# Down-weight sums moved behind the layer norm's scales, z spilled and loaded by halves, transfers reordered

## The chip, the cores and the metric

The kernel runs on one core of one Trainium2 chip. The metric is the device time of one execution in microseconds (us). TensorE (PE), VectorE (DVE), ScalarE (ACT) and GpSimd (POOL) compute; all transfers are issued from SyncE's queue (SP, in the profile SPq), one after the other.

## What is computed

x has 4 batches of 1024 tokens with 512 features. Two layers, each with a residual:

```python
x = x + layernorm(attn(layernorm(x), Wq, Wk, Wv, Wo))
x = x + layernorm(ffn(layernorm(x), gate_cp, up_cp, down_cp))

def attn(x, Wq, Wk, Wv, Wo):     # attention between features, not tokens
    q, k, v = x @ Wq, x @ Wk, x @ Wv
    scores = einsum('bse,bsf->bef', q, k) / sqrt(16)
    return einsum('bef,bsf->bse', softmax(scores), v) @ Wo

def ffn(h, gate_cp, up_cp, down_cp):   # 512 -> 2048 -> 512
    gate_w, up_w, down_w = (spline(cp) for cp in (gate_cp, up_cp, down_cp))
    return (silu(h @ gate_w.T) * (h @ up_w.T)) @ down_w.T
```

The three weights of the second layer are cubic (Catmull-Rom) interpolations of some 8,000 control points each, 1,048,576 values from one line of points. So gate and up are reached over short polynomials of the position: a token's 512 features are first multiplied with 16 position features per tile and per quarter of the input, which gives z, and z with small unit weights gives gate and up. The down weight is 40 columns wide boxes and a few moments, computed on the chip from control points times coefficients, four terms added.

## The kernel before, in words

There are two blocks with a barrier between them.

**The attention block** (`attention_block`, from L63) takes one batch per body: `body(b, True)` for b = 0 to 2 in a hardware loop, then `body(3, False)`, `more` being False. All products are done in a high and a low part (three matmuls for one, `product`, L690). PE's order in a body: chain products of 4 squares each (K = 4 tiles): Gram matrix times Wk, then Wq times that, softmax between, attention times Wo, Wv times that (L761 to L797), then the output of 8 token tiles (NT = 8, L801 to L810), then the Gram matrix of the next batch (`next_gram`). ScalarE evacuates the high part of a bank (`evac_hi`), VectorE the low part (`evac_lo`, L544), and PE waits for the low parts of the chain before the next chain (`lo_done`).

The layer norm of the next batch runs in body b beside the last two chains: VectorE's `ln_step(b + 1, j)` (L535) does for tile j the statistics (`ln_stats`, L517 to L520), for tile j - 1 the normalization (`ln_norm`, L522) and for j - 2 the low part (`ln_lo`, L530), one step behind each `evac_lo`. Between statistics and `ln_norm` GpSimd computes 1 / sqrt(variance + eps) with two tiny operations, `ln_scale` (L333): it waits for `ln_mv` and gives `ln_rstd`, on which `ln_norm` waits. For the output tiles `y_scale` (L341) does the same.

GpSimd also makes weights, in the order of its program (`body`, L387). `unit_weights(c)` (L351) makes the unit weights of the second layer, two of 8 parts per body; `sum_job(b, k)` (L374) makes a sixth (JOBS = 6) of a body's share of the down weight: a multiply of 640 elements per partition (L379) and two additions (L381 of 320, L385 of 160). Before, all six sums and both `unit_weights` of a body stand ahead of its eight `ln_scale`. The jobs' inputs come in two buffers, `load_job(b, k)` (L224), which waits for `job_summed` of two jobs earlier. `job_hi` (L440, ScalarE) and `job_lo` (L555, VectorE) split the sums in the output tiles' loop, and `job_ready` counts them; the store of all of a body's jobs is L290, the last of SP's body.

SP's `body` (L246) holds the order of the transfers: x tiles for the next norm (`load_x`, four buffers), jobs, the stores of the unit weights (`store_units`), then in the loop over t (L272) the stores of x1 (the first layer's output) and the residual loads (`load_res`, L212). In the last body VectorE's `ystats` and residual sums (L619, L630) run as ever, and the first five tiles' z are made: `feats.spill` writes z to DRAM, and at t = 3 `ffn_in.load_z` loads it back, turned so that features are partitions (L284 to L286). One group's z is 2 MB, in two halves of 1 MB. A spill is one transfer of 128 KB (L885 to L887), 16 of them for a group (8 per half, SPILLS = 16).

**The FFN block** (`ffn_block`, from L1031) runs 8 groups of 512 tokens, 16 steps each. A step on PE: gate and up products from z (`gate_up`, L1405), a moment pair, a sixteenth of the previous group's down products (`part`), and in some steps the z of a tile of the next group. ScalarE does silu (L1249, its table load is the only one in this block), VectorE gate times up (L1318), GpSimd the low part (L1204). Before the first step of a group PE waits for z's first half, before step 8 for the second (L1408, `i % HALF == 0`). In quad 2 of 4 of each group SP does `regroup` (L1159): it spills the next group's 16 pieces, then `load_z` (L1022) waits for the first half's spills, loads, waits for the second half's and loads. Behind it in SP's order stand an output store, the reload of a residual buffer, and the load of a token tile (`feats.load`, L878) which VectorE's `stats` (L924) reads a quad later.

## Time and profile before

| | us |
|---|---|
| Median of 3 runs | 849.83 |
| Lowest and highest | 847.49, 853.59 |
| Profiled execution, device time | 854.14 |
| Its span in the profile | 852.4 |
| PE busy | 754.2 (88%) |
| VectorE busy | 522.1 (61%) |
| GpSimd busy | 444.9 (52%) |
| ScalarE busy | 369.4 (43%) |

The attention block takes the first 422 us of the span, of which body 0 begins near 40, body 1 near 138, body 2 near 226 and body 3 near 314; the FFN block takes the rest. A row names the line of the kernel, the engine, and out<-in by tile names; a bracket at its end is the idle time of its engine before it and who ended that. In the waits the name before the arrow is the waiting engine and instruction, the one behind it who released it. PEclk is the granted TensorE clock as a share of 2.4 GHz. Some tiles share memory, so that `z`, `down`, `shared` or `z_lo` in a row of the first block are its weights, residuals and norm parts.

### The profile page before, as it was taken

What the parts mean: (1) busy time and instruction counts of PE and PEld (TensorE: products, weight loads), DVE (VectorE), ACT (ScalarE), POOL (GpSimd) and SP (SyncE); (2) the same over time, 40 slices, a digit from 0 to 9 for tenths busy, and PEclk for the clock granted to TensorE, in tenths of its full rate; (3) what the DMA queues carried; (4) which work ended last, traced back from release to release, by engine and by line L of the source; (5) the groups of instructions that cost most, each with busy time, mean ns of one, the idle gap of its engine ahead of it and who ended that gap; (6) DMA issues with size and microseconds to landing.
All of it is one profiled execution on the core that took longest, in us unless ns stands there. A gap on an engine that the chain in (4) does not pass through costs nothing.

```text
span 852.4 us, 19230 instructions
## 1 busy us (share of the span) xinstructions
PE 754.2 (88%) x7152; PEld 511.4 (60%) x7152; DVE 522.1 (61%) x1025; ACT 369.4 (43%) x632; POOL 444.9 (52%) x616
## 2 busy tenths in 40 slices
PE   5696699999999999799577799989979899998996
PEld 3484476877687768586333465656646556564565
DVE  6553663586448754565466477766757767764553
ACT  2321232333233323233356465655656556665641
POOL 4299547934793479203235344554535545454542
PEclk9798699999999999899779899999999999999999
DMA  8444426521764165405843326262361633516212
GB/s 283 151 161 128 150 88 243 184 94 65 218 206 115 52 202 196 105 1 157 280 143 113 124 74 213 77 222 90 122 202 57 195 122 124 200 65 199 76 61 100
DMA packets 64313, 120.54 MB, mean 141 GB/s; under 512 B 12144, under 2 KB 28656, under 8 KB 62192
## 3 DMA queue, kind: packets, MB, share of 16 engines
q1 hardware_dynamic: 64240, 119.53, 42.9%
q8 instruction: 51, 0.84, 0.4%
q14 instruction: 22, 0.18, 0.1%
HBM read 82.94 MB, written 36.57 MB: 140 GB/s over the span
## 4 chain that ended last, share of the span: by engine, by line
PE 25%; SPq 9%; DMA 7%; DVE 4%; issue 3%; ACT 2%; POOL 0%; DVEq 0%; ACTq 0%
SPq L886 8%; DMA z<-token_features 5%; PE gbank L1417 5%; PE ubank L1417 4%; PE ybank L1458 3%; PE ybank L1459 2%; PE ybank L1460 2%; PE mbank L1433 2%; DMA out<-x_res 1%; PE ybank L1447 1%; DVE inter L1318 1%; PE ybank L1449 1%; PE ybank L1448 1%; PE zbank L974 1%; ACT gated L1249 1%
## 5 line engine op out<-in xcount | busy, mean ns | idle before, releaser
L1204 POOL TENSOR_TENSOR act<-inter,act 128x512 f16<-128x512 f32 x128 | 156.5, 1230 | 154.9 <-ACT act L1245 154.9
L1318 DVE SCALAR_TENSOR_TENSOR inter<-ubank,c_up,gated 128x512 f32<-128x512 f32 x128 | 95.9, 749 | 107.1 <-ACT gated L1249 99.8
L1249 ACT ACTIVATE gated<-gbank,c_gate 128x512 f32<-128x512 f32 x128 | 87.7, 685 | 71.2 <-PE gbank L1417 71.1
L1458 PE MATMUL ybank<-down,act 128*128 128x160 f16 x512 | 111.3, 236 | 0.0
L1459 PE MATMUL ybank<-down,act 128*128 128x160 f16 x512 | 110.4, 235 | 0.0
L1460 PE MATMUL ybank<-down,act 128*128 128x160 f16 x512 | 110.3, 235 | 0.0
L1245 ACT CAST act<-inter 128x512 f16<-128x512 f32 x128 | 78.9, 617 | 47.4 <-DVE inter L1318 47.4
L1417 PE MATMUL gbank<-z,s_twice 128*32 128x512 f16 x512 | 52.9, 403 | 30.4 <-DMA z<-token_features 18.1
L1458 PEld LDWEIGHTS ybank<-down,act 128*128 128x128 f16 x512 | 50.3, 98 | 40.4 <-issue 36.7
L692 PE MATMUL ybank<-ga_hi,xT_hi 128*128 128x512 f32 x128 | 52.8, 412 | 3.8 <-ACT shared L490 1.9
L1417 PE MATMUL ubank<-z,s_twice 128*32 128x512 f16 x512 | 51.9, 395 | 2.7 <-DVE inter L1318 2.7
L345 POOL TENSOR_TENSOR yr<-ymv,eps 128x1 f32<-128x1 f32 x32 | 20.5, 639 | 64.0 <-DVE ymv L622 64.0
L490 ACT ACTIVATE shared<-ybank,yr 128x512 f32<-128x512 f32 x32 | 22.0, 688 | 72.9 <-POOL yr L347 72.9
L1459 PEld LDWEIGHTS ybank<-down,act 128*128 128x128 f16 x512 | 50.6, 99 | 3.9 <-issue 0.3
L547 DVE SCALAR_TENSOR_TENSOR tu_lo<-chain,tu_hi 128x512 fp32r<-128x512 f32 x32 | 22.1, 690 | 50.3 <-ACT tu_hi L432 50.3
L1417 PE MATMUL gbank<-z,s_low 128*32 128x512 f16 x512 | 51.8, 395 | 0.0
L1417 PE MATMUL ubank<-z,s_low 128*32 128x512 f16 x512 | 51.6, 393 | 0.0
L1460 PEld LDWEIGHTS ybank<-down,act 128*128 128x128 f16 x512 | 50.5, 99 | 0.0
L693 PE MATMUL ybank<-ga_lo,xT_hi 128*128 128x512 f32 x128 | 50.1, 392 | 0.0
L694 PE MATMUL ybank<-ga_hi,xT_lo 128*128 128x512 f32 x128 | 50.0, 390 | 0.0
L432 ACT ACTIVATE tu_hi<-chain 128x512 fp32r<-128x512 f32 x32 | 19.1, 596 | 69.9 <-PE chain L694 69.9
L1417 PEld LDWEIGHTS gbank<-z,s_twice 128*32 128x32 f16 x512 | 13.3, 93 | 58.4 <-issue 31.4
(190 smaller groups left out, 2110.4 us busy)
## 6 DMA issues: line engine op xcount, KB each, us to landing
x_ln<-x SPq DMA_DIRECT2D x64, 256.0 KB, 3.5
z<-token_features SPq DMA_DIRECT2D x16, 1024.0 KB, 6.5
job<-job_in SPq DMA_DIRECT2D x24, 640.0 KB, 5.0
shared<-x SPq DMA_DIRECT2D x32, 256.0 KB, 2.7
x<-shared SPq DMA_DIRECT2D x32, 256.0 KB, 2.0
token_features<-z_hi SPq DMA_DIRECT2D x64, 128.0 KB
token_features<-z_lo SPq DMA_DIRECT2D x64, 128.0 KB
x_res<-x SPq DMA_DIRECT2D x32, 256.0 KB, 2.7
```

The source lines that it names most:

```text
L692: pe.matmul(out, l_hi, r_hi, start=start, stop=False)
L693: pe.matmul(out, l_hi, r_lo, start=False, stop=False)
L694: return pe.matmul(out, l_lo, r_hi, start=False, stop=stop)
L886: sp.dma_start(self.spilled[half, part, k].rearrange("f t n -> t f n"), self.z_parts[buf][part][:, half * self.K + k, :]).then_inc(self.z_ ...
L1204: pool.tensor_tensor(hidden[par][:, i, TOK:2 * TOK], inter[:, i % INTERS, :], hidden[par][:, i, 0:TOK], ALU.subtract).then_inc(inter_ready, 1)
L1245: act.copy(hidden[par][:, i, 0:TOK], inter[:, i % INTERS, :]).then_inc(inter_hi_done, 1)
L1249: act.activation(gated[:, slot % 2, :], gbank[:], ACT.Silu, scale=c_gate[:]).then_inc(silu_done, 1)
L1318: dve.scalar_tensor_tensor(out=inter[:, i % INTERS, :], in0=ubank[:], scalar=c_up[:], in1=gated[:, i % 2, :], op0=ALU.mult, op1=ALU.mult). ...
L1417: mm = pe.matmul(bank[rows], part[:, side, c, w, rows], z[par][:, i // 4 * 4 + u, :], start=start, stop=not start)
L1458: pe.matmul(out, hidden[par][:, r, high], box[:, 0], start=False, stop=False)
L1459: pe.matmul(out, hidden[par][:, r, high], box[:, 1], start=False, stop=False)
L1460: mm = pe.matmul(out, hidden[par][:, r, low], box[:, 0], start=False, stop=False)
```

## The change

1. GpSimd, bodies 0 to 2: the order is now `unit_weights`, jobs 0 and 1, `unit_weights`, and then behind the eight `ln_scale` one after the other the multiply of job 2, its additions, the multiply of job 3 and so on to job 5. The last body keeps its order.
2. SP, bodies 0 to 2: jobs 2 and 3 are loaded behind the first `store_units`; jobs 4 and 5 between the x tiles 4 to 7; the next body's jobs 0 and 1 behind them.
3. SP, last body: z's halves are loaded at t = 4 and t = 5, and no longer both at t = 3, so behind the last residual load; the store of the down-weight jobs goes ahead of the last x1 store.
4. ScalarE does one tiny silu at the end of the last body.
5. `regroup` spills one half and loads it, then the other.

```diff
@@ -135,6 +135,7 @@
         srec = sb("srec", [P, K], F32)
         mhalf = sb("mhalf", [P, 1], F32)
         eps = sb("eps", [P, 1], F32)
+        silu_seen = sb("silu_seen", [P, 1], F32)
         carrier = sb("carrier", [P, 1], F32)
 
 
@@ -251,18 +252,26 @@
                     sp.wait_ge(xn_normed, B * NT)
                     for m in range(XR):
                         feats.load(sp, x1_t, m, m)
-                load_job(b, 2)
-                load_job(b, 3)
+                if not more:
+                    load_job(b, 2)
+                    load_job(b, 3)
                 store_units(2 * b, True)
-                load_job(b, 4)
-                load_job(b, 5)
+                if more:
+                    load_job(b, 2)
+                    load_job(b, 3)
+                else:
+                    load_job(b, 4)
+                    load_job(b, 5)
                 store_units(2 * b + 1, more)
                 if more:
+                    load_x(b + 1, XR)
+                    load_x(b + 1, XR + 1)
+                    load_job(b, 4)
+                    load_x(b + 1, XR + 2)
+                    load_x(b + 1, XR + 3)
+                    load_job(b, 5)
                     load_job(b + 1, 0)
                     load_job(b + 1, 1)
-                if more:
-                    for t in range(XR, NT):
-                        load_x(b + 1, t)
                 else:
 
                     sp.wait_ge(s_stored, (2 * B + 1) * 64)
@@ -270,6 +279,9 @@
                     ffn_in.load_units(sp, s_dram, KF)
                     feats.spill(sp, 0, SPILLS // 2, 0)
                 for t in range(NT):
+                    if not more and t == NT - 1:
+                        sp.wait_ge(job_ready, (b + 2) * JOBS)
+                        sp.dma_start(d_dram[b], job_out[:]).then_inc(d_stored, 16)
                     sp.wait_ge(x1_ready, b * NT + t + 1)
                     sp.dma_start(x1_t[b * NT + t], x_res[:, t % XR, :]).then_inc(x1_stored[t % XR], 16)
                     if 1 <= t <= NT - XR:
@@ -281,13 +293,15 @@
                         feats.load(sp, x1_t, XR + t, t)
                     if not more and t < 2:
                         feats.spill(sp, (t + 2) * SPILLS // 4, (t + 3) * SPILLS // 4, 0)
-                    if not more and t == 3:
+                    if not more and t == 4:
                         sp.wait_ge(chain_done, b * CHAIN + 3 * K)
-                        ffn_in.load_z(sp, feats, 0, 0)
+                        ffn_in.load_z(sp, feats, 0, 0, 0)
+                    if not more and t == 5:
+                        ffn_in.load_z(sp, feats, 0, 0, 1)
                 if more:
                     load_res(b + 1, XR - 1)
-                sp.wait_ge(job_ready, held(sp, (b + 2) * JOBS))
-                sp.dma_start(d_dram[held(sp, b)], job_out[:]).then_inc(d_stored, 16)
+                    sp.wait_ge(job_ready, held(sp, (b + 2) * JOBS))
+                    sp.dma_start(d_dram[held(sp, b)], job_out[:]).then_inc(d_stored, 16)
 
             for t in range(XR):
                 load_x(0, t)
@@ -371,30 +385,44 @@
                 pool.wait_ge(unit_step, c * UNIT_STEPS + UNIT_STEPS)
                 pool.tensor_tensor(s_out[:, :, 1], units[:, :, 1], s_out[:, :, 0], ALU.subtract).then_inc(s_ready, 1)
 
-            def sum_job(b, k):
-
-                done, free = held(pool, b * JOBS + k + 1), held(pool, b * JOBS + k + 1)
-                loads = held(pool, (b * (JOBS // 2) + k // 2 + 1) * 16)
-                pool.wait_ge(job_loaded[k % 2], loads)
+            def multiply_job(b, k):
+
+                pool.wait_ge(job_loaded[k % 2], held(pool, (b * (JOBS // 2) + k // 2 + 1) * 16))
                 pool.tensor_tensor(job[:, k % 2, 0], job[:, k % 2, 0], job[:, k % 2, 1], ALU.mult).then_inc(job_mult, 1)
+
+            def add_job(b, k):
+
+                done = held(pool, b * JOBS + k + 1)
                 pool.wait_ge(job_mult, done)
                 pool.tensor_tensor(job[:, k % 2, 0, 0:2], job[:, k % 2, 0, 0:2], job[:, k % 2, 0, 2:4],
                                    ALU.add).then_inc(job_add, 1)
                 pool.wait_ge(job_add, done)
-                pool.wait_ge(job_ready, free)
+                pool.wait_ge(job_ready, done)
                 pool.tensor_tensor(sums[:, k], job[:, k % 2, 0, 0], job[:, k % 2, 0, 1], ALU.add).then_inc(job_summed, 1)
 
+            def sum_job(b, k):
+                multiply_job(b, k)
+                add_job(b, k)
+
             def body(b, more):
-                for c in range(2):
-                    sum_job(b, 2 * c)
-                    sum_job(b, 2 * c + 1)
-                    unit_weights(2 * b + c)
-                sum_job(b, 4)
-                sum_job(b, 5)
                 if more:
+                    unit_weights(2 * b)
+                    sum_job(b, 0)
+                    sum_job(b, 1)
+                    unit_weights(2 * b + 1)
                     for t in range(NT):
                         ln_scale(b + 1, t)
+                        if t % 2 == 0:
+                            multiply_job(b, 2 + t // 2)
+                        else:
+                            add_job(b, 2 + t // 2)
                 else:
+                    for c in range(2):
+                        sum_job(b, 2 * c)
+                        sum_job(b, 2 * c + 1)
+                        unit_weights(2 * b + c)
+                    sum_job(b, 4)
+                    sum_job(b, 5)
                     for m in range(XR):
                         feats.scale(pool, m)
                 for t in range(NT):
@@ -495,6 +523,7 @@
                         job_hi(b, t - 1)
                 if not more:
                     feats.z_high(act, XR, 0, 1, last_banks)
+                    act.activation(silu_seen[:], eps[:], ACT.Silu)
 
             def weight_hi(n):
                 act.wait_ge(w_loaded[n], 16)
@@ -1019,13 +1048,12 @@
             sp.dma_start(self.s_low[0:rows, side], s_dram[1, side]).then_inc(self.s_loaded, 16)
             sp.dma_start(self.s_low[rows:2 * rows, side], s_dram[1, side]).then_inc(self.s_loaded, 16)
 
-    def load_z(self, sp, feats, g, par):
+    def load_z(self, sp, feats, g, par, half):
 
         z = self.z0 if par == 0 else self.z1
-        for half in range(2):
-            sp.wait_ge(feats.z_spilled[half], (g + 1) * feats.SPILLS // 2 * 16)
-            sp.dma_start(z[:, half * self.half:(half + 1) * self.half, :],
-                         feats.spilled[half].rearrange("a k f t n -> (a k f) t n")).then_inc(self.z_loaded[par][half], 16)
+        sp.wait_ge(feats.z_spilled[half], (g + 1) * feats.SPILLS // 2 * 16)
+        sp.dma_start(z[:, half * self.half:(half + 1) * self.half, :],
+                     feats.spilled[half].rearrange("a k f t n -> (a k f) t n")).then_inc(self.z_loaded[par][half], 16)
 
 
 def ffn_block(nc, x1, feats, ffn_in, d_dram, moments, c_gate, c_up, c_out, out, id16):
@@ -1161,8 +1189,8 @@
 
                 for half in range(2):
                     sp.wait_ge(z_loaded[1 - par][half], loads_before * 16)
-                feats.spill(sp, 0, feats.SPILLS, g, 1 - par)
-                ffn_in.load_z(sp, feats, g, par)
+                    feats.spill(sp, half * feats.SPILLS // 2, (half + 1) * feats.SPILLS // 2, g, 1 - par)
+                    ffn_in.load_z(sp, feats, g, par, half)
 
             def quad(g, par, count, j, made, begun, more):
                 if more:
```

## Rows read from the trace of the kernel before

**Rows 1.** Waits of PE, whole span: us in total, times, longest us.

```profile
PE gbank L1417 <- DMA z<-token_features: 18.1, 7, 4.4
...
PE chain L692 <- DVE tu_lo L547: 9.9, 3, 8.2
```

**Rows 2.** Timelines of VectorE and GpSimd, first body: start us, us, instruction.

```profile
70.25 0.90 DVE L593 SCALAR_TENSOR_TENSOR ga_lo<-shared,srec,ga_hi 128x512 fp32r<-128x512 f32 x1
...
89.45 0.55 DVE L527 TENSOR_SCALAR xn<-x_ln,mv,rstd 128x512 f32<-128x512 f32 x1 [14.42 <-POOL rstd L339]
...
110.20 0.70 DVE L619 BATCH_NORM_STATS2 ystats<-ybank 128x6 f32<-128x512 f32 x1 [0.34 <-PE ybank L694]
...
66.95 1.71 POOL L379 TENSOR_TENSOR job<-job 128x640 f32<-128x640 f32 x1
...
74.06 3.09 POOL L357 TENSOR_TENSOR units<-units,ucoef 128x640 f32<-128x640 f32 x2
...
82.42 1.53 POOL L379 TENSOR_TENSOR job<-job 128x640 f32<-128x640 f32 x1
...
87.98 0.52 POOL L385 TENSOR_TENSOR sums<-job 128x160 f32<-128x160 f32 x1
```

**Rows 3.** Windows view, first body: length, busy engines, PEclk, DMA share, GB/s.

```profile
90.60:102.00 11.40, 9.72 (x22) 6.76 (x23) 9.18 (x23) 3.48 (x7) 5.19 (x8) 0.52 0.47 156
```

**Rows 4.** Timeline of VectorE, second body.

```profile
174.60 0.75 DVE L593 SCALAR_TENSOR_TENSOR ga_lo<-shared,srec,ga_hi 128x512 fp32r<-128x512 f32 x1
...
182.49 0.69 DVE L547 SCALAR_TENSOR_TENSOR tu_lo<-chain,tu_hi 128x512 fp32r<-128x512 f32 x1 [0.16 <-ACT tu_hi L432]
...
198.18 0.70 DVE L619 BATCH_NORM_STATS2 ystats<-ybank 128x6 f32<-128x512 f32 x1 [0.34 <-PE ybank L694]
```

**Rows 5.** Timelines of VectorE and of GpSimd where both read SBUF, second body.

```profile
167.26 1.12 DVE L590 TENSOR_SCALAR ga_hi<-shared,srec 128x512 fp32r<-128x512 f32 x1
...
166.53 1.57 POOL L379 TENSOR_TENSOR job<-job 128x640 f32<-128x640 f32 x1
```

**Rows 6.** Timelines of SP's queue, VectorE, ScalarE and PE between the two blocks.

```profile
408.01 0.84 SPq L1027 DMA_DIRECT2D z<-token_features  x2
...
409.73 0.33 SPq L216 DMA_DIRECT2D shared<-x  x1
...
418.41 0.75 DVE L630 SCALAR_TENSOR_TENSOR shared<-shared,yr 128x512 f32<-128x512 f32 x1 [3.84 <-DMA shared<-x]
...
414.41 0.69 ACT L490 ACTIVATE shared<-ybank,yr 128x512 f32<-128x512 f32 x1 [1.71 <-POOL yr L347]
...
422.92 1.28 ACT L1249 ACT_TABLE_LOAD   x1 [5.68 <-PEq L84]
...
423.49 0.67 PE L1417 MATMUL gbank<-z,s_low 128*32 128x512 f16 x4
```

**Rows 7.** Timelines of SP's queue and of VectorE at one of seven regroupings.

```profile
509.63 0.65 SPq L886 DMA_DIRECT2D token_features<-z_lo  x1
...
515.68 3.95 SPq L1027 DMA_DIRECT2D z<-token_features  x2
...
528.14 0.43 SPq L878 DMA_DIRECT2D x_ln<-x  x1
...
536.03 0.70 DVE L924 BATCH_NORM_STATS2 hstats<-x_ln 128x6 f32<-128x512 f32 x1
```

**Rows 8.** Timeline of PE: first and last of seven waits for z.

```profile
472.95 0.62 PE L1417 MATMUL gbank<-z,s_twice 128*32 128x512 f16 x4 [4.42 <-DMA z<-token_features]
...
781.45 0.62 PE L1417 MATMUL gbank<-z,s_twice 128*32 128x512 f16 x4 [3.60 <-DMA z<-token_features]
```

**Rows 9.** Windows of 8 us behind each z wait; the third of seven.

```profile
573.50:581.50 8.00, 7.97 (x84) 5.35 (x85) 1.55 (x3) 2.77 (x5) 1.89 (x2) 0.63 0.64 231
```

**Rows 10.** The page's DMA issues, us from issue to landing last.

```profile
z<-token_features SPq DMA_DIRECT2D x16, 1024.0 KB, 6.5
...
x<-shared SPq DMA_DIRECT2D x32, 256.0 KB, 2.0
```

## The prediction, made before any run of the changed kernel

> **What bounds the kernel now.** I read the page first (share of busy time, 40 slices), then PE's waits, then the timelines and windows around the long ones. PE is busy 88% of the span and is the pace almost everywhere: where it runs it runs back to back, so only its gaps and its stretches at half clock can be won. Its long waits [rows 1] are 18.1 us in 7 waits for z in the second block and 9.9 us for the low part of a chain product; a third gap, at the change of blocks, shows in ScalarE's 5.7 us too [rows 6]. The changed lines touch all three.
>
> The second is one event of body b = 0. VectorE has the statistics of the first token tile, then stands 14.42 us (from 75.03) for the rstd of GpSimd and starts at 89.45; GpSimd stood in its down-weight sums until 88.5 [rows 2]. PE waits 8.2 of these 14.4 us and then runs on at a mean granted clock of 0.52, so almost all at 1.2 instead of 2.4 GHz, for 11.4 us [rows 3]. From VectorE's last softmax operation (70.25) to the first output statistics (110.20) the first body takes 39.95 us; the second takes 198.18 - 174.60 = 23.58 us for the same work [rows 2, 4]. So 16.4 us are lost there, and only in b = 0, where GpSimd must first split the weights wo and wvT and comes late to its sums.
>
> **First part: the sums between the scales (bodies 0 to 2).** The work is the same; four of six sums per body (multiply, two additions) move behind the eight `ln_scale`. In the first body sums 2 to 5 are two pairs, 66.95 to 74.06 and 82.42 to 88.50, with unit weights between [rows 2]: 7.1 + 6.1 = 13.2 us. Without them norm 0 starts at 89.45 - 13.2 = 76.2. The statistics are ready at 75.0, so it is still 1.2 us late.
>
> Then there is a cost. In this stretch VectorE has a step each 2.72 us with 0.16 us idle in it [rows 4]: it is full. Behind each scale GpSimd now has a multiply (1.57 us) or two additions (0.9 and 0.5). Where a VectorE operation reads two operands or one fast operand of SBUF while GpSimd does the same, the trace shows them after each other: the softmax scaling at 167.26 took 1.12 us (others 0.49) and ended 0.3 us after GpSimd's multiply of 166.53 to 168.10 [rows 5]. ln_norm and ln_lo are such operations. I went through the eight steps with these durations: the multiply, begun after the last step's `pow`, ends about 0.4 us after norm would start, so each of seven steps grows by some 0.1 to 0.2 us, and in bodies 1 and 2 the first output statistics come 1.1 us late (bounds: 0.3 if the idle time takes it, 7 if each step is lengthened by a full us). In body 0 come on top the 1.2 us of late start and the first multiply, which starts together with norm 0 (up to 1.57, taken as 1.5); with some 1.5 from the later steps that is a lag of 4.2. Gain of body 0: 16.4 - 4.2 = 12.2 us (bounds 7 and 15.5); loss of bodies 1 and 2: 2 x 1.1 = 2.2. The softmax of bodies 1 and 2 has GpSimd to itself then, which saves VectorE 1 us, but its next step waits for PE's next product: worth nothing.
>
> The Trainium skill ("SBUF — State Buffer", "SBUF: two separate sides") says that VectorE and GpSimd share one port pair as an exclusive lock, held for the whole instruction, the loser blocked. The row above agrees. Taken strictly, for all of each instruction, it speaks against this part; by it the sum would be that of the second rival.
>
> SP's queue: loads 4 and 5 and the x tiles are interleaved. load_job(4) needs sum 2, done about 2.7 us after norm 0, and is followed by the x load for tile 6, wanted 9 us later; nothing late. Loads of units come behind the first unit weights, 8 us ahead of use. In the last body sums stay ahead: no change.
>
> **Second part: the change of blocks.** Before, both z loads (2 MB) are issued at 408.01, the last residual load behind them at 409.73, and VectorE's last residual sum waits 3.84 us for it, to 418.41; its other operand was ready at 414.41 + 0.69 = 415.1 [rows 6]. Now that load goes ahead of z (about 408.5, landed by 412), so the sum starts at 415.1: 3.3 us earlier. The sum's store follows at 415.9; the down store, before the last of all, goes ahead of it at 414. But both stand behind 2 MB of z in the queue, issued at 409.5 and 411.4 and so landed near 418.5. So the end of the block moves by less than 3.3: I take 2.5 us (bounds 0 and 3.3). The early silu takes the table load (1.28 us from 422.92, to 424.20) out of the second block, but the gate products that the silu needs end at 423.49 + 0.67 = 424.16 [rows 6]: worth 0.04 us, nothing. If the start were faster by more than that, it would be worth up to 1.3. In the old block it ends at 418.8, before SP.
>
> **Third part: z by halves.** Before, each of seven regroupings issues 16 spills, then both z loads. The eighth spill is issued at 509.63, the first load at 515.68, 6.05 us later [rows 7]. Now the load waits for the landing of those eight. A store of 256 KB (the page's x from shared) lands 2.0 us after its issue [rows 10]; the last spill before took at most 4.2, as the second load could go 3.6 us after the first [rows 7]. I take 2.7, nearer to the store since nothing is queued behind it: the first half is issued 3.3 us earlier (1.85 to 4.05). Its own time stays at the row's 6.5 us: fewer spills ahead, eight behind. So z lands 3.3 us earlier. Of the seven waits only the first (4.42) and the last (3.60) exceed that [rows 8]; they keep 1.1 and 0.3. Gain 18.1 - 1.4 = 16.7 us.
>
> PE is at half clock after the four waits of 2.9 us and more, and not after the three of 1.9 and less. Mean clock 0.63 over 8 us [rows 9] is 2 x 0.37 x 8 = 5.9 us at half; the other three such stretches give 4.0, 3.4 and 2.7. Together 16.0 us at half, that is 8.0 us of PE's work. With 1.1 us of wait left nothing falls: 8.0 us gained. FFN: 24.7.
>
> The second half's load now comes some 6 us later than before but is needed eight steps of 3 us after the first: covered. SP leaves the regrouping 2.6 us later; behind it stand the output store, its reload and the x_ln load of 528.14, read at 536.03 [rows 7]. It lands in 3.5, so 4.4 us of cover less 2.6 and less the wait PE no longer has (1.5 here): just enough. If gone, it costs the difference, about 1 us per group.
>
> **Sum.** 12.2 - 2.2 + 2.5 + 16.7 + 8.0 = 37.2 us. The profiled execution took 854.14 (span 852.4): 816.9. It stands 4.3 above the median 849.83, so on the median's scale 812.6; I say 813.
>
> **Rivals.** (a) Spills land slowly, or SP's lateness delays x_ln. With 4.2 us for landing, z comes 1.85 earlier, five waits shrink by that, the 1.5 and 0.9 go: 11.65 us, and one clock fall stays (2 of 8). FFN 17.6, total 820. For: the 4.2 was seen. Against: that spill had 1 MB behind it.
>
> (b) Mutual waiting of GpSimd and VectorE paces the token steps. GpSimd needs per step 1.4 for the scale and 1.5 for the sum, VectorE's two operations 1.2; if none overlap, 4.1 less what needs no port (0.4) is 3.7 and not 2.72. Seven steps: 7 us per body. Body 0 then gains 16.4 - 1.2 - 7 = 8.2, bodies 1 and 2 lose 14. Against the forecast's 10.0 that is 15.8 worse: 828. For: rows 5. Against: statistics and products read from PSUM run beside GpSimd unhindered.
>
> (c) Slower: the first half's read is in flight with eight spills' writes and its landing takes longer than the 6.5 us. Each us later than before costs 7 us of wait, and three more waits pass 2.9 and fall to half clock, 2 us each. The other parts bring 12.5, so it decides from 1.0 us later than before on (7 + 6 = 13); at 2 us later it is 14 + 6 - 12.5 = 7.5 slower: 857. It needs about 11.8 us from issue to landing where the median is 6.5 [rows 10]. Against: before, the last spills and the second load surrounded it as well.
>
> (d) It does not do what it says: z is not what PE waits for next, but the chain ACT - VectorE; then the waits change their name. Only 12.5 and part of the clock remain: about 835. Against: PE ran without gaps between z waits.
>
> **Chances.** Forecast 0.62, (a) 0.20, (b) 0.11, (c) 0.03, (d) 0.04. Below the forecast the bounds give 15.5 + 3.3 + 18.1 + 8 - 0.6 = 44 us, 805; above, (b) and (a) reach 828 to 835. Range 804 to 829. A measurement of this kernel can tell about 1%. Faster by over 1%: forecast, (a), (b) and most of (d), 0.95; within 1%: 0.02; slower: 0.03.
>
> **What would show it.** Right: PE's waits list shows z with about 1.5 us and tu_lo with under 3; VectorE's wait for rstd falls from 14.4 to 1 to 2; body 0 from the last softmax operation to the first output statistics about 28 us, bodies 1 and 2 about 24.7; no residual wait of 3.8; PEclk near 1.0 behind the regroupings; the first z load about 2.7 us after the eighth spill. Wrong: VectorE waiting for x_ln, ln_norm or ln_lo of over 1 us each, or PE's z waits as long as before.

## The result, and the profile after

The changed kernel takes 829.93 us (median of 6 runs, 818.71 to 833.93) beside 851.71 us for the kernel before (6 runs): a ratio of 0.969 (95% interval 0.964 to 0.973). That ratio leaves out the three slow ones of the six runs (832.26 to 833.93, over 1.5% above the fastest); the medians of all six give 0.974. The profiled execution took 827.61 us (span 825.8) where the one before took 854.14 (span 852.4). The forecast was 816.9 on this scale: the direction is right, 10.7 us of the forecast gain of 37.2 are missing.

I cut the span in three, in each trace: up to the first spill of z, from there to PE's first gate product, and the second block. The last row has, for the second block, the time that PE idles and the time at half clock, 2 x (1 - PEclk) x length, summed over the block. The two overlap where PE stands idle at half clock:

```
                            before   after   gain   forecast
up to the first spill        386.6   374.5   12.1   12.2 - 2.2 = 10.0
change of blocks              36.5    38.4   -1.9    2.5
second block                 429.3   412.9   16.4   24.7
  PE idle / half clock   46.3/40.1  36.3/23.8
```

Counted in the same clock records only while PE works, half clock fell from 29.9 to 16.2 us. Half of that difference, 6.9, and the 10.0 us of idle time make 16.9 us, where the block is 16.4 shorter.

PE's waits, of the whole span (us in total, times, longest). The z waits of [rows 1], 18.1 us, have no row any more. In their place the wait for the low part of hT, which was 3.8 us, stands at 11.6:

```profile
PE chain L721 <- DVE ga_lo L622: 12.8, 10, 3.6
PE zbank L1003 <- DVE hT L970: 11.6, 14, 3.8
PE gbank L1445 <- PEq L84: 8.9, 1, 8.9
...
PE gbank L1445 <- issue: 2.4, 1, 2.4
```

First body, VectorE and then GpSimd (start us, us, instruction). GpSimd leaves the unit weights at 74.2, gives the rstd, and VectorE's norm 0 starts at 75.16 instead of at 89.45 [rows 2]. From the last softmax operation to the first output statistics: 97.14 - 70.22 = 26.9 us, before 39.95:

```profile
70.22 1.10 DVE L622 SCALAR_TENSOR_TENSOR ga_lo<-shared,srec,ga_hi 128x512 fp32r<-128x512 f32 x1
...
75.16 1.68 DVE L556 TENSOR_SCALAR xn<-x_ln,mv,rstd 128x512 f32<-128x512 f32 x1
...
97.14 0.69 DVE L648 BATCH_NORM_STATS2 ystats<-ybank 128x6 f32<-128x512 f32 x1
...
73.53 0.68 POOL L386 TENSOR_TENSOR s_out<-units,s_out 128x256 f16<-128x256 f32 x1
...
75.01 1.55 POOL L391 TENSOR_TENSOR job<-job 128x640 f32<-128x640 f32 x1
```

Second body, the same two engines: 185.53 - 161.38 = 24.15 us, before 23.58 [rows 4]. The norms beside a multiply take 0.64 and 0.78 us, not 0.53; both end 0.29 us after that multiply does (169.52 + 1.57 = 171.09, and 171.38):

```profile
161.38 0.75 DVE L622 SCALAR_TENSOR_TENSOR ga_lo<-shared,srec,ga_hi 128x512 fp32r<-128x512 f32 x1
...
170.74 0.64 DVE L556 TENSOR_SCALAR xn<-x_ln,mv,rstd 128x512 f32<-128x512 f32 x1
...
176.18 0.78 DVE L556 TENSOR_SCALAR xn<-x_ln,mv,rstd 128x512 f32<-128x512 f32 x1
...
183.65 1.01 DVE L556 TENSOR_SCALAR xn<-x_ln,mv,rstd 128x512 f32<-128x512 f32 x1
184.58 1.02 DVE L561 SCALAR_TENSOR_TENSOR z_lo<-xn,z_hi 128x512 f16<-128x512 f32 x1
185.53 0.69 DVE L648 BATCH_NORM_STATS2 ystats<-ybank 128x6 f32<-128x512 f32 x1
...
169.52 1.57 POOL L391 TENSOR_TENSOR job<-job 128x640 f32<-128x640 f32 x1
...
175.11 1.56 POOL L391 TENSOR_TENSOR job<-job 128x640 f32<-128x640 f32 x1
```

Change of blocks, SP's queue and then VectorE, ScalarE and PE. The residual load (397.72) now goes ahead of z, and VectorE's wait for it fell from 3.84 to 1.81 us [rows 6]. The last x1 store goes out at 405.02 behind 2 MB of z; SP stands 6.8 us for its landing and starts the second block's transfers only at 412.73. The silu of the second block starts at 414.01, right behind the gate products' end, 413.30 + 0.67 = 413.97:

```profile
397.72 0.33 SPq L217 DMA_DIRECT2D shared<-x  x1
398.15 0.37 SPq L1055 DMA_DIRECT2D z<-token_features  x1
...
399.24 0.48 SPq L1055 DMA_DIRECT2D z<-token_features  x1
...
405.02 0.33 SPq L286 DMA_DIRECT2D x<-shared  x1
412.73 0.34 SPq L907 DMA_DIRECT2D x_ln<-x  x1
...
404.24 0.75 DVE L659 SCALAR_TENSOR_TENSOR shared<-shared,yr 128x512 f32<-128x512 f32 x1 [1.81 <-DMA shared<-x]
...
414.01 0.69 ACT L1277 ACTIVATE gated<-gbank,c_gate 128x512 f32<-128x512 f32 x1 [7.86 <-PE gbank L1445]
...
413.30 0.67 PE L1445 MATMUL gbank<-z,s_low 128*32 128x512 f16 x4
```

The regrouping that answers to [rows 7], SP's queue: first spill, eighth spill, z's first half, last spill, second half, output store, its reload, x_ln's load. SP stands 4.06 us for the landing of the eighth spill (488.44 to 497.49 is 9.05 us to the first load; before, 11.26) and 5.98 us for that of the last. It is through 508.84 - 488.44 = 20.4 us after the first spill; before, after 11.26 + 3.95 = 15.2 [rows 7]. Then the reload waits 6.0 us for the output store's landing:

```profile
488.44 0.58 SPq L915 DMA_DIRECT2D token_features<-z_hi  x1
...
493.43 0.57 SPq L915 DMA_DIRECT2D token_features<-z_lo  x1
497.49 0.33 SPq L1055 DMA_DIRECT2D z<-token_features  x1
...
502.48 0.57 SPq L915 DMA_DIRECT2D token_features<-z_lo  x1
508.46 0.33 SPq L1055 DMA_DIRECT2D z<-token_features  x1
508.84 0.85 SPq L1177 DMA_DIRECT2D out<-x_res  x1
514.83 0.33 SPq L1173 DMA_DIRECT2D x_res<-x  x1
515.21 0.43 SPq L907 DMA_DIRECT2D x_ln<-x  x1
```

What comes of it a little later, in three groups (7.0 us of VectorE's waits in all), here behind the next regrouping: the x_ln load goes out at 565.27, VectorE waits 3.45 us for it, PE 3.78 us for what follows from it. Timelines of SP, VectorE and PE:

```profile
565.27 0.34 SPq L907 DMA_DIRECT2D x_ln<-x  x1
...
570.37 0.69 DVE L953 BATCH_NORM_STATS2 hstats<-x_ln 128x6 f32<-128x512 f32 x1 [3.45 <-DMA x_ln<-x]
...
571.92 0.29 PE L1003 MATMUL zbank<-hT,feat 128*128 128x128 f16 x1 [3.78 <-DVE hT L970]
```

Two falls of the clock are left between start and tail of the second block: one right behind that wait, 2 x 0.43 x 4 = 3.4 us at half, and one of 3.4 us behind a single "issue" wait of 2.4 us (a wait for which the profile shows no cause). The second is not new: the kernel before has one too, 2 x 0.28 x 6 = 3.4 us, behind an "issue" wait of 3.7 us. The first of these in the windows view (length, busy PE, PEld, DVE, ACT, POOL, then PEclk, DMA share, GB/s), and then that of the kernel before:

```profile
571.00:575.00 4.00, 3.08 (x32) 2.62 (x36) 2.81 (x6) 0.62 (x1) 3.40 (x4) 0.57 0.49 158
```

```profile
636.00:642.00 6.00, 5.63 (x56) 2.86 (x57) 3.05 (x5) 2.44 (x5) 0.00 (x0) 0.72 0.31 92
```

### The profile page after: what moved, and what is told of

Same layout as the page of the kernel before. It is cut to its first block and busy times, and to the rows that moved or that the text cites. A ratio compares the mean times of both kernels' runs of the same rounds, so it can differ in the third digit from the quotient of the medians.

```text
span 825.8 us, 19227 instructions
## 1 busy us (share of the span) xinstructions
PE 741.8 (90%) x7152; PEld 507.0 (61%) x7152; DVE 531.3 (64%) x1025; ACT 369.6 (45%) x633; POOL 444.3 (54%) x616
## 5 line engine op out<-in xcount | busy, mean ns | idle before, releaser
L1232 POOL TENSOR_TENSOR act<-inter,act 128x512 f16<-128x512 f32 x128 | 158.3, 1246 | 130.4 <-ACT act L1273 130.3
L1486 PEld LDWEIGHTS ybank<-down,act 128*128 128x128 f16 x512 | 50.1, 98 | 39.2 <-issue 35.5
L460 ACT ACTIVATE tu_hi<-chain 128x512 fp32r<-128x512 f32 x32 | 19.1, 598 | 76.3 <-PE chain L723 76.3
L359 POOL TENSOR_TENSOR yr<-ymv,eps 128x1 f32<-128x1 f32 x32 | 20.4, 639 | 59.3 <-DVE ymv L651 59.3
L1377 DVE SCALAR_TENSOR_TENSOR x_res<-y,orr,x_res 128x512 f32<-128x512 f32 x32 | 42.9, 1339 | 10.8 <-ACT y L1295 7.7
```

The costliest lines, as they stand in the source:

```text
L1232: pool.tensor_tensor(hidden[par][:, i, TOK:2 * TOK], inter[:, i % INTERS, :], hidden[par][:, i, 0:TOK], ALU.subtract).then_inc(inter_ready, 1)
L1377: dve.scalar_tensor_tensor(out=x_res[:, q % 2, :], in0=y[:, q % 2, :], scalar=orr[:, q, 2:3], in1=x_res[:, q % 2, :], op0=ALU.subtract, op ...
L1486: pe.matmul(out, hidden[par][:, r, high], box[:, 0], start=False, stop=False)
```

## The experiments

Ratios are to the kernel before, which took 851 to 852 us in each series. The four runs a1 to a4 are one series on one chip; e1c to e3c and b1 to b4 ran on another chip, without the changed kernel beside them. The parts of each trace, in us:

```
                            to first spill  change  2nd block  PE idle/half clock in it
before                           386.6       36.5     429.3      46.3 / 40.1
after                            374.5       38.4     412.9      36.3 / 23.8
e1c sums only                    375.4       36.4     429.2      43.6 / 43.6
e2c change of blocks only        385.6       38.0     435.1      48.9 / 45.9
e3c halves only                  386.3       36.3     414.3      36.7 / 25.1
a1 after again                   373.4       37.3     412.6      34.0 / 26.9
a2 x_ln load ahead               375.3       36.6     403.7      30.0 / 14.5
a3 second half of z last         374.2       33.7     407.0      29.9 / 21.4
a4 both                          375.0       35.9     405.1      31.5 / 12.6
b1 twelve spills                 375.1       36.2     415.0      37.3 / 25.9
b2 twelve, x_ln ahead, z last    374.9       35.5     413.4      37.1 / 20.9
b3 without the silu              375.3       37.6     410.3      33.7 / 21.2
b4 short sums                    373.6       36.1     412.0      36.7 / 16.1
```

How far one trace can be trusted is seen where the code is the same. The change of blocks has the code of the changed kernel in seven traces (after, e2c, a1, a2, b1, b3, b4) and takes 36.1 to 38.4 us. The half clock in the second block is 16.1 to 26.9 us in four traces that differ there by the silu's table load at most (after, a1, b3, b4). Much of that spread lies at the start of the block: mean clock of its first 14 us 0.56 in a1, 0.77 in b4.

**One part at a time, on the kernel before.** First the sums alone (the order of SP's loads, changed with them, is not shown):

```diff
+                    unit_weights(2 * b)
+                    sum_job(b, 0)
+                    sum_job(b, 1)
+                    unit_weights(2 * b + 1)
                     for t in range(NT):
                         ln_scale(b + 1, t)
+                        if t % 2 == 0:
+                            multiply_job(b, 2 + t // 2)
+                        else:
+                            add_job(b, 2 + t // 2)
```

> The kernel before with the first part alone (the down-weight sums of bodies 0 to 2 behind the token scales, and SP's loads in that order). Forecast's terms: 12.2 gained in body 0, 1.1 lost in each of bodies 1 and 2, so 10.0 us faster, ratio 0.988. What the trace of the changed kernel suggests: about 13 gained in body 0 and 0.3 lost in each of the others, 12 us faster, ratio 0.986. Rival (b), mutual waiting of GpSimd and VectorE at 3.7 us a step: 8.2 gained, 14 lost, 6 us slower, ratio 1.007. If the gains of the parts add up, the second block takes the same time as in the kernel before.

841.62 us, ratio 0.9865 (0.982 to 0.991), so 11.5 us faster. The stretch up to the first spill is 11.2 shorter, the rest is the same to 0.2. PE's wait for z stays, seven times and 16.4 us.

Next the change of blocks alone (shown are z's loads; the down-weight store and the early silu move with them):

```diff
-                    if not more and t == 3:
+                    if not more and t == 4:
                         sp.wait_ge(chain_done, b * CHAIN + 3 * K)
-                        ffn_in.load_z(sp, feats, 0, 0)
+                        ffn_in.load_z(sp, feats, 0, 0, 0)
+                    if not more and t == 5:
+                        ffn_in.load_z(sp, feats, 0, 0, 1)
```

> The kernel before with the second part alone (residual load and down-weight store ahead of z's first loads, these at t = 4 and t = 5, silu seen in the last body). Forecast: 2.5 us faster (bounds 0 and 3.3), ratio 0.997. Theory from the changed kernel's trace: the last x1 store now stands behind 2 MB of z in the queue and lands as late as before or later; the wait of VectorE for the residual falls by 2 us and comes back as SP's wait for that store: 0 to 2 us slower, ratio 1.000 to 1.002, and the last x1 store takes over 6 us to land.

853.46 us (12 runs), ratio 1.0017 (0.999 to 1.004): the forecast gain of 2.5 us, a ratio of 0.997, is not there, and a loss is not resolved either. The change of blocks is 1.5 us longer in the trace, and SP's wait for the last x1 store is the longest seen:

```profile
SPq L321 <- DMA x<-shared: 7.6, 1, 7.6
```

The second block's 5.8 us more in this trace (waits for z and the clock) don't show in the timed ratio, so I read nothing from them.

Then the regrouping by halves alone:

```diff
                 for half in range(2):
                     sp.wait_ge(z_loaded[1 - par][half], loads_before * 16)
-                feats.spill(sp, 0, feats.SPILLS, g, 1 - par)
-                ffn_in.load_z(sp, feats, g, par)
+                    feats.spill(sp, half * feats.SPILLS // 2, (half + 1) * feats.SPILLS // 2, g, 1 - par)
+                    ffn_in.load_z(sp, feats, g, par, half)
```

> The kernel before with the third part alone (each half of z loaded behind its own eight spills). Forecast: 24.7 us faster, ratio 0.971, waits of PE for z of 1.4 us in all. Theory from the changed kernel's trace: z waits gone, but SP is 5 us later behind each regrouping, VectorE waits for the x_ln load in three groups and for a reload once, PE waits some 8 us more for the low part of hT, one or two clock falls stay: 16 us faster, ratio 0.981. Rival (c), z landing later than before: slower.

838.53 us, ratio 0.9853 (0.981 to 0.989), 12.5 us faster; in the trace the second block is 15.0 shorter. PE's waits, and VectorE's in the second block: z is gone but for 0.3 us, hT stands at 11.5 where it was 3.8, and VectorE waits for x_ln five times:

```profile
PE zbank L975 <- DVE hT L942: 11.5, 13, 3.8
...
PE gbank L1417 <- DMA z<-token_features: 0.3, 1, 0.3
```

```profile
DVE hstats L925 <- DMA x_ln<-x: 7.7, 5, 3.5
```

So the missing part of the FFN's gain comes with this edit alone. The three parts add up to -11.5 + 1.4 - 12.5 = -22.6 us, where the changed kernel measures 0.969 and 0.973 in two series, 26.7 and 22.8 us faster: the sum fits the second, and the first within the intervals, which are some 4 us wide to either side.

**What holds the second block.** The changed kernel again, and three edits of it, in one series on one chip. The x_ln load of quad 3 ahead of the regrouping:

```diff
-                if more:
-                    m = g * Q + j + AHEAD + 2
+                for ahead in {2: (2, 3), 3: ()}.get(j, (j,)) if more else ():
+                    m = g * Q + ahead + AHEAD + 2
```

> The changed kernel once more, as the yardstick of this call: 0.969 of the time of the kernel before, some 830 us; PE waits for the low part of hT near 12 us in all, VectorE for the x_ln load of quad 3 in two or three groups.

> The changed kernel with the x_ln load that quad 3 issues behind the regrouping issued ahead of it, in quad 2. If SP's lateness behind the regrouping is what took the third part's missing 8 us, the waits of VectorE for that load go, PE's waits for the low part of hT fall from 11.6 to about 4 us and a clock fall or two with them: 6 to 10 us faster than the changed kernel (ratio to it 0.988 to 0.993). Rival: the load is late anyway or another step of the chain (reload, statistics) takes its place: within 2 us of it. By a second rival it is slower, as the load takes transfer time from the spills and z lands later: z waits of PE come back.

The changed kernel: 827.48 us, ratio 0.973 (0.968 to 0.978). With the load ahead: 818.41 us, ratio 0.964 (0.959 to 0.969), 9 us faster than the changed kernel. VectorE has no wait for x_ln left, and PE's waits are:

```profile
PE zbank L1003 <- DVE hT L970: 4.4, 13, 1.5
...
PE gbank L1445 <- DMA z<-token_features: 1.1, 2, 0.6
```

hT is at 4.4 (8.5 in the changed kernel of this series, 11.6 in its first profile), z at 1.1 us: the transfer put ahead of the spills costs z next to nothing. Neither rival fits: the kernel is faster, and no other wait took the place of this one. So SP's lateness through the x_ln load is shown as a cause.

Its size is less sure than the 9 us. Idle PE and half clock in the second block fell by 4.0 and 12.4 us. Of the 12.4, 6.8 are two falls of 3.4 us each behind the two x_ln waits of a1; these and the idle time are worth 4.0 + 6.8 / 2 = 7.4 us. Another 5.6 lie at the start of the block, which the edit does not touch, and where b4, without an edit there, is at 0.77 like a2. The first 14 us of the block in a1 and in a2:

```profile
410.70:424.70 14.00, 10.95 (x96) 4.76 (x96) 7.68 (x16) 5.71 (x10) 3.78 (x6) 0.56 0.80 245
```

```profile
411.90:425.90 14.00, 9.24 (x96) 4.29 (x96) 7.96 (x16) 6.12 (x11) 3.90 (x7) 0.76 0.82 248
```

The second half of group 0's z behind the last x1 store:

```diff
-                    if not more and t == 5:
+                    if not more and t == NT - 1:
                         ffn_in.load_z(sp, feats, 0, 0, 1)
```

> The changed kernel with the second half of group 0's z loaded behind the last x1 store instead of before it. If the 1 MB ahead of that store is what makes it late (6.8 us to its landing), it lands in 3 to 4 us and the second block starts 3 us earlier: 3 us faster (ratio to the changed kernel 0.996). Rival: the first half alone fills the queue just as long, or the second half is then wanted before it is there: 0 to 2 us slower, with a z wait of PE in the first group.

819.04 us, ratio 0.964 (0.959 to 0.969). SP's queue: the last x1 store (403.58) now has its second half of z behind it, and the second block's first load goes out at 407.76, 4.2 us behind the store and not 7.7:

```profile
398.08 0.37 SPq L1055 DMA_DIRECT2D z<-token_features  x1
...
403.58 0.33 SPq L286 DMA_DIRECT2D x<-shared  x1
403.96 0.45 SPq L1055 DMA_DIRECT2D z<-token_features  x1
407.76 0.34 SPq L907 DMA_DIRECT2D x_ln<-x  x1
```

The change of blocks is 33.7 us, below all seven traces with the changed kernel's code there (36.1 to 38.4). The two other traces with this edit have 35.9 (a4) and 35.5 (b2), and SP waits 2.8, 4.7 and 4.6 us for the store in the three, 5.7 to 7.6 in the seven. So the direction of the theory is shown, but its 3 us are not: the change of blocks is 3.6 us shorter than in a1 here, but only 0.7 shorter in a4 than in a2, and 0.7 in b2 than in b1. And the kernel gained 8 us: 5.6 lie in the second block, where VectorE waits for x_ln once for 1.2 us and not twice for 4.3, though the regrouping's own times are unchanged (x_ln's load 25.6 to 27.7 us after the first spill, 26.0 to 28.4 in the changed kernel). I did not find what shifts VectorE's reading of that tile against the load. It does say that the x_ln load is late by a few us at most, and that its waits come and go with small shifts.

Both edits together:

> Both of these edits. If their gains are of different places they add up: 9 to 13 us faster than the changed kernel, about 818 us. If the start of the second block only moves a wait into the first regrouping, no more than the edit of the x_ln load alone gives.

816.86 us (813.96 to 817.84), ratio 0.960 (0.956 to 0.964). It is the fastest here and has the narrowest spread, but the gains don't add up: with x_ln ahead, nothing was left in the second block for the other edit (405.1 us, 403.7 with the load ahead alone).

**Less waiting of SP in the regrouping.** Twelve spills ahead of the load of the first half, on the changed kernel:

```diff
                 for half in range(2):
-                    sp.wait_ge(z_loaded[1 - par][half], loads_before * 16)
-                    feats.spill(sp, half * feats.SPILLS // 2, (half + 1) * feats.SPILLS // 2, g, 1 - par)
+                    for last in ((8, 12), (16,))[half]:
+                        if last < 16:
+                            sp.wait_ge(z_loaded[1 - par][last // 12], loads_before * 16)
+                        feats.spill(sp, first, last, g, 1 - par)
+                        first = last
                     ffn_in.load_z(sp, feats, g, par, half)
```

> The changed kernel with twelve spills ahead of the load of z's first half in each regrouping, and not eight: SP issues four more spills in the time in which it now stands for the landing of the eighth. Theory: SP's lateness costs through the x_ln load, so with SP out of the regrouping some 3 us earlier (spill start to second z load 17 us and not 20) and z's first half issued as early as now, the waits of VectorE for x_ln go and PE's waits for the low part of hT fall from 8.5 to 11.6 to about 5 us: 4 to 8 us faster than the changed kernel (ratio to it 0.990 to 0.995). Rival: with twelve spills queued ahead of it the first half is issued or lands later, and waits of PE for z of 1 to 2 us in each of several groups come back: no faster.

825.38 us, ratio 0.969 (0.965 to 0.972): within the interval of the changed kernel. The rival was right in that z is waited for again. SP issues z's second half 17.7 to 19.1 us after the first spill and not 19.3 to 20.8, and x_ln's waits fall to 1.4 us in all; but four more spills stand in front of z's first half, which lands in 5.9 us (median) where the changed kernel's landed in 5.5, and PE's z waits are back:

```profile
PE gbank L1449 <- DMA z<-token_features: 5.4, 5, 2.1
PE zbank L1003 <- DVE hT L970: 5.3, 13, 1.1
PE gbank L1449 <- issue: 4.9, 1, 4.9
```

The last row is a second loss that the rival did not have: the "issue" wait is 4.9 us, 2.1 in a1 (4.7 in the next run, 2.2 in a4). Idle PE is 3.3 us more than in a1: z 4.8 and "issue" 2.8 more, hT 3.2 less, the rest 1.1 less. Nothing here shows whether the edit makes the "issue" wait longer; it is 3.7 us in the kernel before and in b4.

The same with the two edits of before:

> The same, with the x_ln load of quad 3 ahead of the regrouping and the second half of group 0's z behind the last x1 store. If the x_ln load was all that SP's lateness held up, no faster than those two edits alone (817 us); if the output store and its reload behind it matter too, 2 to 4 us faster than they.

827.61 us, ratio 0.971 (0.967 to 0.976), 1.3% slower than those two edits without the twelve (another series, whose kernel before differs by 0.3 us). Here z is waited for 7.0 us in 6 groups (2.3 with the two edits alone), and nothing is left to pay for it; the "issue" wait is 2.5 us longer. Neither expectation had a slower kernel. VectorE's waits for the reload, 2.9 us with the two edits alone, are gone here; what that is worth can't be told beside the z waits.

**Two terms of the sum by themselves.** Without the early silu:

```diff
                     feats.z_high(act, XR, 0, 1, last_banks)
-                    act.activation(silu_seen[:], eps[:], ACT.Silu)
```

> The changed kernel without the silu of one column in the last body, so that ScalarE loads silu's table in the second block. Forecast: the early silu is worth 0.04 us, as PE's gate products end when the table load does: ratio to the changed kernel 1.000. Rival: the start of the second block is PE's, ScalarE is late for it and the load of 1.3 us shows in full: 1.3 us slower, below what this comparison can tell, but seen in the profile as a wait of PE or VectorE for ScalarE behind the first gate products.

824.43 us, ratio 0.970 (0.965 to 0.975), no difference. ScalarE's timeline has the table load in the second block again, and the silu starts at 414.04 instead of 414.01, with the gate products' end at 413.97 in both traces:

```profile
412.74 1.28 ACT L1276 ACT_TABLE_LOAD   x1 [7.01 <-PEq L84]
414.04 0.69 ACT L1276 ACTIVATE gated<-gbank,c_gate 128x512 f32<-128x512 f32 x1
```

And the sums behind the token scales cut to 4 of 160 columns. This kernel leaves out the other 156, so that its output is not the layer's:

```diff
-                            multiply_job(b, 2 + t // 2)
+                            multiply_job(b, 2 + t // 2, 4)
                         else:
-                            add_job(b, 2 + t // 2)
+                            add_job(b, 2 + t // 2, 4)
```

> The changed kernel with the sums behind the token scales of bodies 0 to 2 made on 4 of 160 columns, so their instructions, waits and loads stand where they were but occupy GpSimd and the port hardly at all (most of those down-weight columns are left out of the computation; sums is set to zero once at the start). If the sums beside ln_norm and ln_lo cost what the changed kernel's trace shows, body 0 from the last softmax operation to the first output statistics falls from 26.9 to about 24 us and bodies 1 and 2 from 24.2 to 23.6: 4 us faster. Forecast's terms: 4.2 less the 1.2 of late start, and 1.1 in each of two: 5.2 us. Rival, that the sums there are free: 1 us or less.

826.82 us, ratio 0.971 (0.966 to 0.977), no difference to be measured. In the trace bodies 1 and 2 take 23.59 and 23.58 us (changed kernel 24.15 and 24.11) and body 0 takes 97.81 - 71.07 = 26.74 (26.92), although its norm 0 takes 0.55 us now and not 1.68:

```profile
71.07 1.09 DVE L623 SCALAR_TENSOR_TENSOR ga_lo<-shared,srec,ga_hi 128x512 fp32r<-128x512 f32 x1
...
76.00 0.55 DVE L557 TENSOR_SCALAR xn<-x_ln,mv,rstd 128x512 f32<-128x512 f32 x1
...
97.81 0.70 DVE L649 BATCH_NORM_STATS2 ystats<-ybank 128x6 f32<-128x512 f32 x1 [0.35 <-PE ybank L724]
```

The sums beside the norms cost 0.2 + 0.6 + 0.5 us in the traces, nearer to the rival's bound of 1 us than to the forecast's 5.2. The timed ratio alone could not tell these apart.

## Why the prediction was right, and where it was off

**The gain of body 0** was 13.0 us against 12.2 (bounds 7 and 15.5). Norm 0 came at 75.16, forecast 76.2; a load of the prologue had landed 1.2 us sooner in this execution, and GpSimd was earlier by about that, which is luck. The first multiply did collide with the norm, 1.68 us. But this cost next to nothing: the short sums leave 26.7. The rest of the lag, 26.7 less 23.6 in the later bodies, lies ahead of the second chain product's split, which comes 1.0 + 2.1 us later than in bodies 1 and 2 and waits for ScalarE and so for PE, in a stretch that PE begins at a granted clock of 0.50 (window from 70.2 to 75). It isn't the sums; that it is the clock is argued, not tried.

**The loss of bodies 1 and 2** was mis-sized: 0.57 us late at the first output statistics, 1.1 forecast, and only 0.33 a body at the last residual sum. The norms grow by 0.1 to 0.4 us (0.64, 0.67, 0.78, 0.80, 0.89 where 0.53 is undisturbed), but the 0.16 us of idle time in each step takes most of it, and the steps stay at 2.72 to 2.74 us, one of 2.83 apart. Most of the 0.57 us falls behind the last `evac_lo`: the norm there takes 1.01 us and the low part 1.02, and from its start (183.05) to the first output statistics (185.53) pass 2.48 us, where b4 needs 2.09. Rival (b), 3.7 us a step, is refuted by the sums-only run, 11.5 us faster where it wanted 6 slower. Rival (c) falls with the halves-only run: z is not late. Rival (d), that the waits change their name, holds in part: of z's 18.1 us, 7.8 came back as waits for the low part of hT, though behind a late load and not from the chain of ScalarE and VectorE by itself.

**The change of blocks** is the one wrong sign in this trace: -1.9 for +2.5, and below my bound of 0. In the seven traces with this code it is 36.1 to 38.4 us against 36.3 to 36.5 without: from 0.4 shorter to 1.9 longer, 0.8 longer in the mean. That the gain is missing is shown, a loss is not. The prediction named the cause ("both stand behind 2 MB of z in the queue") and then took a landing "near 418.5" for the store, as if the sum's 3.3 us came through nearly whole. SP stood 6.8 us for this store of 256 KB behind 2 MB, where such a store lands 2.0 us after its issue [rows 10] and the last one before cost SP 1.2. The bound at nothing was unfounded: before, the store went out 10.8 us behind z's second load (408.42, 419.19), now 5.8 us behind it (399.24, 405.02). The blocks-only run (no gain) and the second half moved behind the store (0.7 to 3.6 us shorter) show that this order costs. The silu was worth 0.03 us, forecast 0.04: that part of the step held.

**z by halves** was right in mechanism and overrated in the net. Three terms: (1) the landing of the eighth spill, taken as 2.7 with a bound of 4.2: it is 3.6 to 5.4, median 4.1. That is the first half of rival (a). So at the regrouping shown the first load comes 2.2 us earlier and not 3.3. (2) Its own time, held at 6.5: the page has 5.5. Together 3.2 us, as forecast (3.3), by two errors that cancel, which is luck; all z waits went, the 1.4 us that should have been left too. (3) SP's lateness. "SP leaves the regrouping 2.6 us later": it is 5.2 here. The last spill goes out 14.04 - 10.64 = 3.4 us later, and then takes 6.0 us to land with z's first half in flight (4.2 before): 1.8 more, which the forecast didn't have. The cover of the x_ln load, "just enough", was gone, and "about 1 us per group if gone" was 3.45, 2.80 and 0.73 in three groups, with another 3.06 for one reload. Behind the longest the clock fell as well, for 3.4 us at half; the prediction had such a fall only behind z waits. That is the second half of rival (a), to which I gave 0.20, and the prediction's own sign of being wrong: VectorE waiting for x_ln over 1 us. The x_ln load put ahead gives 9.0 us back in the second block, of which some 7 can be traced to it; 8.3 were missing.

Of the 8.0 us of clock, 6.9 came. Half clock while PE works fell by 13.7 us: the 16.0 behind z waits went, one new fall of 3.4 (3.1 with PE at work) came behind the wait for hT, and the start of the block has 0.9 less. The fall behind the "issue" wait stayed; the prediction had overlooked it. Its line between waits of 2.9 us, behind which the clock fell, and of 1.9, behind which it did not, is one of that trace: in the changed kernel no fall follows the hT wait of 3.13 us at 675.59 (mean clock 1.00 from 675 to 681), and in the sums-only run one follows a z wait of 1.99 us at 613.15 (0.72 from 612 to 618).

The total: 0.969 of the median before, 849.83, is 823 us, in the upper half of the range of 804 to 829, 10 above the forecast. The median of all six runs, 829.93, lies just above the range. By time alone rival (a), 820, is nearer than the forecast of 813. What happened is the forecast's main mechanism, PE no longer waiting for z, with (a)'s lateness and a missing gain at the change of blocks on top, and 2.1 us more than forecast from the first part.

## What to carry to other kernels

When a wait is put between transfers on a queue's engine, follow everything that this engine issues next with the full landing time under load, and not the landing time of a quiet store; then ask for each such transfer how much cover it has: how long before its reader needs it it would land. A cover that is "just enough" is where the next bound sits. What has slack to spare (here a load wanted 30 us later, whose buffer is free) goes ahead of the wait. And a small transfer on whose landing a stage ends should not be queued behind a megabyte that nobody wants yet.

## What the runs showed of the hardware

A VectorE norm that meets a GpSimd multiply on SBUF ends 0.27 to 0.29 us after the multiply, wherever it began: started 0.15 us into it, it took 1.68 us; started 0.35 us before the multiply's end, 0.64; 0.49 us before, 0.78. Alone it takes 0.53. A low part beside an addition (184.58 above, the addition 184.46 to 185.06) took 1.02 us and not 0.68, and ended 0.54 behind it. So some 0.25 us of the instruction are hidden in the wait, and a collision costs that much less than "one after the other" would have it. The Trainium skill ("SBUF — State Buffer", "SBUF: two separate sides") has the loser blocked until the winner's end; the ends agree with that, and the price per step is the part above.

A spill of 128 KB behind seven others landed 3.6 to 5.4 us after its issue, and with a read of 1 MB in flight 5.7 to 6.7 us. For the last x1 store SP waited 5.7 to 7.6 us with 2 MB of z close ahead of it in seven traces, 2.8 to 4.7 in the three with one of the two MB behind it, and 1.2 in the three with z issued 10.2 us or more ahead of it (before, sums only, halves only). A 1 MB read of z landed in 5.5 us behind eight landed spills, in 5.9 with four more in flight, and in 6.5 behind sixteen.
